# Window attention by quads of four images, with its norm in the loop and its result added to x on the chip

## The chip, the cores and the metric

The program runs on one core of a Trainium2 chip. The metric is the device time of one execution, in microseconds; the time before is the median of three runs. PE is the matrix engine, DVE the vector engine, ACT the activation engine, POOL the general engine; SP and ACT also start DMAs. Each engine works off its own list of instructions in order, and semaphores order the engines among each other. Matrix products land in PSUM, eight banks of 512 f32 columns on 128 lanes.

## The reference

x is f32, 16 images of 24 channels, 56 x 56 pixels. Four layers follow each other; each adds a mixer's result to x and then a feed-forward network's result. Only the first mixer, the norm in front of it and the feed-forward of layer 0 are touched here:

```python
x = x + _L0_conv_ref(_ln_c(x), w_qkv, pos_emb, w_out, b_out)     # attention in 7 x 7 windows
t = _to_tokens(x)
t = t + _L0_ffn_ref(_ln_t(t), W1, b1, W2, b2)                    # rounded to e5m2 and f16
...
# _ln_c: minus the mean, by the standard deviation, over the 24 channels of a pixel
# _L0_conv_ref, per window of 49 pixels and each of 3 heads of 32:
dots = einsum(q, k) * scale + bias[head]                         # 49 x 49
out  = einsum(softmax(dots), v)                                  # then w_out, b_out
```

The other mixers are a selective scan (layer 1), a scan in four directions (layer 2) and an LSTM over rows (layer 3).

## The kernel before

All of x stays in SBUF for the whole program as 128 lanes of J x 3136 columns: lane group g (32 lanes, 24 of them used) holds images g*4 to g*4+3 one after the other. N = 392 columns are 7 rows of 56 pixels, a strip; a chunk of the normalization and of the feed-forward is one strip of four images, one per lane group, and there are 32 of them.

`first_norm_phase` (lines 508 to 644) loads x by 16 DMAs, clears the rest of the lanes, and normalizes 32 chunks with four rings of buffers: PE subtracts the mean by a matrix (L630), ACT squares (L599), PE averages (L637), ACT takes the logarithm and the exponential (L605, L611), DVE multiplies into a padded tile (L585), and SP stores four pieces per chunk to `normed` in DRAM (L559).

`attention_phase` (lines 682 to 1000) takes one image at a time: 128 chunks of 7 rows, 8 windows each. SP loads 24 channels of 7 rows from `normed` (L761); POOL copies them window by window into `xw`, 24 lanes of 128 (L785), after a small instruction that orders it (L780). Under the 24 lanes, lanes 32 to 80 of `xw` hold a one-hot and those of `keys` the position bias, so the product of both over 128 lanes gives scores and bias at once. On PE a chunk is: the keys of three heads (L821, one product of 392 columns), the values of each window (L829, 16 products of 48 columns that alternate between two halves of 64 lanes), the weighing of the values of the chunk two before (L863 and L865, 16 products of 49 columns), the scores (L840, 8 products of 147 columns, windows alternating between the two halves), and the transposes of the probabilities of the chunk before (L851, L853). DVE takes maxima (L958), subtracts (L961), sums (L974), takes reciprocals (L977), lands part of the transposed (L969) and the result with its bias (L983); ACT lands keys (L893), values (L901) and the rest of the transposed (L912), takes exponentials (L906) and stores the result to `mixed` in DRAM (L917); POOL multiplies by the shares (L792). Two buffers of most tiles alternate; the function `slots` writes a prologue, a loop of two chunks a turn, and an epilogue, and the order of calls in each engine's `slot` is the order of its work.

In the trace an f32 matmul is two instructions, a transpose one, and each has its own weight load (PEld).

`feed_forward_phase` (lines 131 to 502) runs once per layer over the 32 chunks, four chunks a turn. SP loads the mixer's result into four `mixed` buffers (L217), POOL adds it to x (`add_mixed`, L360) four chunks ahead and adds the network's result (`update`, L366) when `biased` (L321) is there; DVE rounds and casts (L292 to L315), ACT normalizes, and SP stores the next mixer's normalized input (L243). The order on SP is: store of chunk c, then the loads of chunk c + 6. PE multiplies zeros at the start (L426) and its mean product of chunk c (L441) waits for `added`.

## Time and profile before

| | us |
|---|---|
| median of three runs (3751.98 to 3758.53) | 3753.66 |
| profiled execution, first to last instruction (span) | 3742.5 |
| PE busy, share of the span | 3205.8, 86% |
| DVE | 2806.7, 75% |
| ACT | 2516.9, 67% |
| POOL | 1935.3, 52% |

The span of the profiled execution is 11.2 us shorter than the median of the runs; what lies around it is not in the trace. The kernel passes through stages one after another, so the shares of the whole span say little about one of them. The touched stages end at 1011.5 us. A matmul's duration in the trace includes the time until its last column has landed, so two that follow each other overlap; busy time counts the overlap once.

### The profile page before, as it was taken

How to read it: one execution, taken by the hardware profiler on the slowest of the kernel's cores; microseconds unless marked ns; L12 is line 12 of the kernel's file. 1: busy time of each engine (PE TensorE's matmuls, PEld its weight loads, DVE VectorE, ACT ScalarE, POOL GpSimd, SP SyncE). 2: the span in 40 equal slices, each digit the busy share in tenths (PEclk: the TensorE clock that was granted, in tenths of full speed). 3: DMA queues.
4: the chain of work that ended last, by engine and by line, in shares of the span. 5: the costliest groups of instructions: out<-in, count | busy, mean ns of one | idle time of the engine just before them, and what ended most of it. 6: DMA issues, size and time to landing. Idle time of an engine off the chain costs nothing. (4 is left out here: it accounts for less than half of the span.)

```text
span 3742.5 us, 70954 instructions
## 1 busy us (share of the span) xinstructions
PE 3205.8 (86%) x21002; PEld 1807.7 (48%) x21002; DVE 2806.7 (75%) x4339; ACT 2516.9 (67%) x4557; POOL 1935.3 (52%) x1754
## 2 busy tenths in 40 slices
PE   5799999989787899999999867887999968788877
PEld 2588888864333444444444322333334324377742
DVE  2566666658636999999999997785999968644467
ACT  4455555548676998989998743785767638644456
POOL 0233333323246888889898875333777763200035
PEclk9899999999898999999999999998999989899999
DMA  4100000012256566574747542220000002230022
GB/s 97 30 15 14 14 15 14 14 26 52 71 168 170 144 182 188 160 209 142 211 138 208 140 120 60 56 55 23 21 22 20 20 24 51 72 70 17 17 53 61
DMA packets 211925, 297.93 MB, mean 80 GB/s; under 512 B 68990, under 2 KB 189106, under 8 KB 211382
## 3 DMA queue, kind: packets, MB, share of 16 engines
q1 hardware_dynamic: 204254, 286.98, 28.5%
q10 hardware_dynamic: 7512, 9.16, 0.9%
q8 instruction: 60, 0.98, 0.1%
q14 instruction: 99, 0.81, 0.1%
HBM read 193.93 MB, written 102.03 MB: 79 GB/s over the span
## 5 line engine op out<-in xcount | busy, mean ns | idle before, releaser
L1773 POOL TENSOR_TENSOR mam_hc<-mam_h,mam_cs 128x896 f32<-128x896 f32 x336 | 703.4, 2094 | 166.8 <-DVE mam_h L1692 93.5
L1692 DVE TENSOR_TENSOR_SCAN mam_h<-mam_a,mam_kept,mam_dbx 128x448 f32<-128x448 f32 x672 | 738.3, 1129 | 41.9 <-ACT mam_a L1562 40.9
L1415 PE MATMUL mam_ps_y<-mam_hc,mam_ident 128*128 128x448 f32 x1344 | 569.6, 557 | 125.2 <-POOL mam_hc L1773 124.9
L1562 ACT ACTIVATE mam_a<-mam_ft,mam_a_neg 128x448 f32<-128x448 f32 x672 | 410.8, 660 | 76.7 <-DVE mam_h L1692 75.6
L1415 PEld LDWEIGHTS mam_ps_y<-mam_hc,mam_ident 128*128 128x128 f32 x1344 | 248.5, 192 | 424.7 <-POOL mam_hc L1773 216.2
L792 POOL TENSOR_TENSOR att_prob<-att_prob,att_share 128x588 f32<-128x588 f32 x128 | 151.7, 1185 | 452.1 <-DVE att_share L977 452.1
L1679 DVE TENSOR_TENSOR mam_dbx<-mam_ps_u,mam_bs 128x448 f32<-128x448 f32 x672 | 381.3, 612 | 0.0
L2196 POOL TENSOR_TENSOR scan_ch<-scan_h,scan_cs 128x392 f32<-128x392 f32 x192 | 262.1, 1379 | 61.9 <-DVE scan_h L2138 57.5
L366 POOL TENSOR_TENSOR all_x<-all_x,f_yb 128x392 f32<-128x392 f32 x128 | 128.0, 1000 | 237.2 <-DVE f_yb L321 237.2
L360 POOL TENSOR_TENSOR all_x<-all_x,f_mixed 128x392 f32<-128x392 f32 x128 | 152.5, 1191 | 181.8 <-DMA f_mixed<-mixed 123.6
L912 ACT ACTIVATE att_pt<-att_ps_t 128x512 f32<-128x512 f32 x128 | 76.5, 598 | 209.9 <-PE att_ps_t L853 209.9
L401 ACT ACTIVATE f_h<-f_hid 96x784 f16<-96x784 f32 x256 | 203.1, 808 | 4.5 <-PE f_hid L459 4.3
L893 ACT ACTIVATE att_keys<-att_ps_keys 24x392 f32<-24x392 f32 x384 | 187.0, 487 | 23.0 <-PE att_ps_keys L821 20.0
L2017 PE MATMUL scan_ps_in<-scan_xin,scan_w_in 128*128 128x392 f32 x512 | 189.0, 513 | 12.1 <-DMA scan_xin<-normed 5.4
L354 POOL MEMSET f_squares_ln<- 128x392 f32 x4 | 1.7, 425 | 366.8 <-POOLq L2282 329.6
L863 PE MATMUL att_ps_out<-att_pt,att_vals 128*24 128x49 f32 x2048 | 189.5, 208 | 2.1 <-ACT att_pt L912 2.1
L865 PE MATMUL att_ps_out<-att_pt,att_vals 128*24 128x49 f32 x2048 | 187.3, 207 | 0.0
L2330 PE MATMUL lstm_ps<-lstm_hs,lstm_w_h 64*128 64x224 f32 x1344 | 143.1, 358 | 50.8 <-DVE lstm_hs L2411 50.8
L2029 PE MATMUL scan_ps_merged<-scan_ch,scan_w_merge 64*128 64x392 f32 x768 | 157.7, 521 | 26.8 <-POOL scan_ch L2196 26.8
L310 DVE CAST f_h<-f_hr 96x1568 fp8e5<-96x1568 f16 x128 | 173.3, 1354 | 5.5
L829 PEld LDWEIGHTS att_ps_vals<-att_nvals,att_xw 128*64 128x64 f32 x4096 | 130.5, 138 | 75.5 <-issue 75.5
L983 DVE TENSOR_SCALAR att_result<-att_ps_out,att_b_out 24x392 f32<-24x392 f32 x128 | 78.6, 614 | 115.9 <-PE att_ps_out L865 115.9
(252 smaller groups left out, 7870.8 us busy)
## 6 DMA issues: line engine op xcount, KB each, us to landing
mam_taps<-normed SPq DMA_DIRECT2D x220, 130.5 KB
mam_bs<-dram_bc SPq DMA_DIRECT2D x56, 448.0 KB, 8.8
mam_cs<-dram_bc SPq DMA_DIRECT2D x56, 448.0 KB, 12.0
mam_ft<-dram_steps SPq DMA_DIRECT2D x42, 448.0 KB, 4.8
normed<-f_staged SPq DMA_DIRECT2D x384, 38.1 KB
f_mixed<-mixed SPq DMA_DIRECT2D x384, 36.8 KB
mam_gt<-dram_gs SPq DMA_DIRECT2D x48, 224.0 KB, 2.7
dram_gs<-mam_gs SPq DMA_DIRECT2D x47, 224.0 KB, 2.6
```

The source lines that it names most:

```text
L310: dve.tensor_copy(h8[p][:], hr[:], saturate=False).then_inc(ff["hidden8"], 1)
L401: act.activation(h16[:, 2 * a:2 * a + 2, :], hid[a][0:HID, :, 0:N], ACT.Copy).then_inc(ff["hidden16"], 1)
L863: pe.matmul(ps_out[0:C, cols], vals[p][:, win, 0:C], pt[p][:, q, 64 * half:64 * half + T], start=True, stop=False)
L865: mm = pe.matmul(ps_out[0:C, cols], vals[p][:, win, C:2 * C], pt2[p][:, q, 64 * half:64 * half + T], start=False, stop=True)
L893: o = act.activation(keys[p][0:C, :, h * T:(h + 1) * T], ps_keys[32 * h:32 * h + C, 0:N].rearrange("c (w t) -> c w t", w=WINS), ACT.Copy)
L1415: mm = pe.matmul(ps_y[p % 2][:, 0:MT], ident[:], hc[t % 2][:, i, :], start=False, stop=(t % 8 == 7 and i == 1))
L1562: act.activation(a[t % 3][:, i, :], ft[p % 2][:, 0, :], ACT.Exp, scale=a_neg[:, at:at + 1]).then_inc(decays, 1)
L1679: dve.tensor_tensor(dbx[:, i, 0:MT], ps_u[:, 0:MT], bs[:, held_row(p // DB, pair) + i, :], ALU.mult).then_inc(driven, 1)
L1692: dve.tensor_tensor_scan(h[:, n % 8, :], a[t % 3][:, i, :], dbx[:, i, 0:MT], kept[:, at:at + 1], ALU.mult, ALU.add).then_inc(scanned, 1)
L1773: pool.tensor_tensor(hc[t % 2][:], h[:, row:row + 2, :], cs[:, 2 * pair:2 * pair + 2, :], ALU.mult).then_inc(weighed, 1)
L2017: pe.matmul(ps_in[i][:, 0:N], w_in[:, i, :], xin[p][:, :, 1:SIDE + 1], start=True, stop=True).then_inc(projected, 1)
L2196: pool.tensor_tensor(out, hd, in_order(cs, 1 - half, d, k), ALU.mult).then_inc(weighed, 1)
```

## The change

The phase of the first norm is gone. Attention loads x itself, from an array that the host has laid out by lanes with its padding, in six pieces of 1, 1, 2, 4, 8 and 16 chunks. It takes the 32 chunks of the other phases: a strip of four images at once, each in its own 32 lanes. A unit is half a chunk, four windows of each of four images, so there are 64 units of 16 windows. Norm, keys and windows of chunk c + 1 and c + 2 are made within the units of chunk c. DVE writes the normalized strip straight into the windows `xw`. Keys are one product per head over all lanes, by weights that are zero outside an image's own lanes. Bias and scores are separate products that add up in the same bank; scores and values use 32 lanes of rows and 64 of columns, weighing 64 of rows and 32 of columns. DVE adds the result and its bias to x in SBUF; no result is stored, and nothing is loaded back.

`feed_forward_phase` gets no `mixed` in layer 0 (`in_place`): no loads, no `mixed` buffers, no `add_mixed`, and its mean products don't wait for `added`. The counts of semaphores are shifted to fit.

The diff, cut to its core (the three `slot` functions are those of PE, ACT and DVE, in this order):

```diff
-        first_norm_phase(nc, x, normed, w)
-        for layer in range(LAYERS):
+        attention_phase(nc, w, x, normed)
+        feed_forward_phase(nc, x, None, normed, out_rows, w, st, 0)
+        for layer in range(1, LAYERS):
...
+        ps_s = buf.psum("ps_s", [P, G, BANK])
+        ps_t = [buf.psum(f"ps_t{i}", [P, BANK]) for i in range(2)]
+        ps_l = [buf.psum(f"ps_l{i}", [P, BANK]) for i in range(2)]
...
+        def outs(side):
+            return ps_t[side][:, HEADS * P:HEADS * P + QW * WIN]
...
+                def scores(u, c, e, q):
+                    for g in range(G):
+                        if g % 2 == 0:
+                            reached(pe, shifted, u * 2 + (g // 2 - 1))
+                        lanes = slice(64 * (g % 2), 64 * (g % 2) + TP)
+                        pe.matmul(ps_s[:, g, 0:SCORES], onehot[lanes, :], bias[lanes, :],
+                                  start=True, stop=False)
+                    pe.wait_ge(keys_sb, c * HEADS + HEADS)
+                    for side in range(2):
+                        for g in range(G):
+                            lanes = slice(32 * g, 32 * g + 32)
+                            for half in range(2):
+                                win = 4 * e + 2 * side + half
+                                mm = pe.matmul(
+                                    ps_s[64 * half:64 * half + TP, g, 0:SCORES].rearrange(
+                                        "i (h a j) -> i h a j", h=HEADS, a=2)[:, :, side, :],
+                                    xw[q][lanes, win, :],
+                                    keys[q][lanes, win, :].rearrange("c (h j) -> c h j", h=HEADS),
+                                    start=False, stop=(side == 1))
+                    mm.then_inc(scored, 1)
...
+                def values_product(e, q):
+                    for half in range(2):
+                        for g in range(G):
+                            lanes = slice(32 * g, 32 * g + 32)
+                            for side in range(2):
+                                win = 4 * e + 2 * side + half
+                                at = SCORES + half * VALUES
+                                mm = pe.matmul(
+                                    ps_s[64 * side:64 * side + TP, g, at:at + VALUES],
+                                    xw[q][lanes, win, :], nvals[lanes, :], start=True, stop=True)
...
+                def weigh_values(e, i):
+                    for half in range(2):
+                        for h in range(HEADS):
+                            for g in range(G):
+                                for side in range(2):
+                                    lanes = slice(64 * side, 64 * side + TP)
+                                    mm = pe.matmul(
+                                        outs(side)[32 * g:32 * g + C].rearrange(
+                                            "c (r s) -> c r s", r=WIN)[
+                                                :, :, half * WIN:(half + 1) * WIN],
+                                        vals[i][lanes, g, half, h * C:(h + 1) * C],
+                                        pt[e][lanes, g * HEADS + h, half, :].rearrange(
+                                            "j (r s) -> j r s", r=WIN),
+                                        start=(h == 0), stop=(h == HEADS - 1))
...
+                def turn_probabilities(u, e, g):
+                    if g == 0:
+                        reached(pe, added, u)
+                        pe.wait_ge(normal, u * 2 + 1)
...
+                def slot(u, c, e, q, on):
+                    if on[2]:
+                        scores(u, c, e, q)
+                    if on[4]:
+                        await_probabilities(u - 2)
+                    if on[2]:
+                        values_product(e, q)
+                    if on[4]:
+                        weigh_values(e, (2 * q + e + 2) % 4)
+                    if on[0]:
+                        subtract_mean(c + 2, q)
+                    if on[1]:
+                        keys_product(c + 1, 1 - q, 0)
+                    if on[3]:
+                        turn_probabilities(u - 1, 1 - e, 0)
+                        turn_probabilities(u - 1, 1 - e, 1)
+                    if on[0]:
+                        variance(c + 2, q)
+                    if on[1]:
+                        keys_product(c + 1, 1 - q, 1)
+                    if on[3]:
+                        turn_probabilities(u - 1, 1 - e, 2)
+                        turn_probabilities(u - 1, 1 - e, 3)
+                    if on[1]:
+                        keys_product(c + 1, 1 - q, 2)
+                    if isinstance(u, int) and u == 1:
+                        for piece in range(len(PIECES) - 1):
+                            pe.wait_ge(x_in[piece], 16)
...
+                def slot(u, c, e, q, on):
+                    if on[2]:
+                        take_values(u, 2 * q + e)
+                    if on[0]:
+                        square(c + 2, q)
+                    if on[1]:
+                        take_keys(c + 1, 1 - q, 0)
+                    if on[3]:
+                        take_turned(u - 1, 1 - e, 0)
+                        take_turned(u - 1, 1 - e, 1)
+                    if on[1]:
+                        take_keys(c + 1, 1 - q, 1)
+                    if on[2]:
+                        exponentials(u, e)
+                    if on[0]:
+                        inverse_deviation(c + 2, q)
+                    if on[3]:
+                        take_turned(u - 1, 1 - e, 3)
+                    if on[1]:
+                        take_keys(c + 1, 1 - q, 2)
...
+                def slot(u, c, e, q, on):
+                    if on[3]:
+                        sums(u - 1, 1 - e)
+                    if on[1]:
+                        window(c + 1, 1 - q)
+                    if on[2]:
+                        find_maximum(u, 0)
+                    if on[4]:
+                        add(u - 2, c - 1, e)
+                    if on[2]:
+                        find_maximum(u, 1)
+                        subtract_maximum(u, e, 0)
+                        subtract_maximum(u, e, 1)
+                    if on[3]:
+                        take_turned(u - 1, 1 - e)
```

on[0] holds in every odd unit, on[1] in every even one; the loop's turn is four units. `reached` waits until a semaphore has a value, and does nothing for a constant of zero or less.

## Rows read from the trace of the kernel before

**Rows 1.** Windows by stage: stretch and length, each engine's busy us (instructions), clock, DMA.

```profile
0.00:109.60 109.60, 54.44 (x128) 23.62 (x128) 25.19 (x40) 46.29 (x97) 5.56 (x6) 0.94 0.40 93
109.60:125.30 15.70, 3.90 (x46) 2.66 (x46) 6.16 (x15) 1.48 (x3) 1.50 (x6) 0.50 0.21 59
125.30:821.70 696.40, 690.71 (x11492) 573.24 (x11488) 478.55 (x768) 403.52 (x765) 242.75 (x506) 1.00 0.06 14
821.70:1011.50 189.80, 162.21 (x630) 74.30 (x630) 143.91 (x304) 146.43 (x257) 65.12 (x65) 0.97 0.22 54
```

**Rows 2.** Waits of attention, the longest: us in total, times, longest.

```profile
POOL att_prob L792 <- DVE att_share L977: 452.1, 128, 8.2
```

**Rows 3.** Timeline of PE in one chunk: start us, duration us, instruction, count.

```profile
400.97 0.25 PE L865 MATMUL att_ps_out<-att_pt,att_vals 128*24 128x49 f32 x2
401.15 1.22 PE L840 MATMUL att_ps_scores<-att_keys,att_xw 128*64 128x147 f32 x16
402.30 0.33 PE L851 MATMUL att_ps_t<-att_ident,att_prob 128*128 128x128 f32 x1
...
403.12 0.27 PE L853 MATMUL att_ps_t<-att_ident,att_prob 128*64 128x128 f32 x1
403.23 0.82 PE L821 MATMUL att_ps_keys<-att_xw,att_mkeys 128*96 128x392 f32 x2
403.98 1.14 PE L829 MATMUL att_ps_vals<-att_nvals,att_xw 128*64 128x48 f32 x32
```

**Rows 4.** Groups by form, 400 to 800 us: busy us, mean ns of one.

```profile
L792 POOL TENSOR_TENSOR att_prob<-att_prob,att_share 128x588 f32<-128x588 f32 x74 | 87.7, 1185 | 258.4 <-DVE att_share L977 258.4
...
L974 DVE TENSOR_REDUCE att_total<-att_prob 128x12 f32<-128x588 f32 x75 | 57.5, 766 | 14.4 <-ACT att_prob L906 14.4
L961 DVE TENSOR_TENSOR att_prob<-att_ps_scores,att_top 128x588 f32<-128x588 f32 x74 | 57.2, 773 | 2.5
L958 DVE TENSOR_REDUCE att_top<-att_ps_scores 128x12 f32<-128x588 f32 x74 | 57.0, 770 | 36.9 <-PE att_ps_scores L840 36.9
L906 ACT ACTIVATE att_prob<-att_prob 128x588 f32<-128x588 f32 x74 | 52.7, 712 | 0.0
L969 DVE COPY att_pt<-att_ps_t 64x512 f32<-64x512 f32 x74 | 49.8, 672 | 0.0
...
L983 DVE TENSOR_SCALAR att_result<-att_ps_out,att_b_out 24x392 f32<-24x392 f32 x74 | 45.4, 614 | 66.9 <-PE att_ps_out L865 66.9
...
L977 DVE RECIPROCAL att_share<-att_total 128x12 f32<-128x12 f32 x75 | 17.1, 228 | 2.6
```

**Rows 5.** Bins of 10 ns: PE instructions in flight, first L840, then L863.

```profile
136.54:136.55 0.01, 0.00 (x1) 1.00 0.00 0
136.55:136.56 0.01, 0.01 (x2) 1.00 0.00 0
...
405.05:405.06 0.01, 0.01 (x1) 1.00 0.00 0
405.11:405.12 0.01, 0.01 (x2) 1.00 0.00 0
```

**Rows 6.** Timeline of PE in one row of the LSTM.

```profile
3400.83 2.55 PE L2330 MATMUL lstm_ps<-lstm_hs,lstm_w_h 64*128 64x224 f32 x24 [0.93 <-DVE lstm_hs L2411]
```

**Rows 7.** Timeline of PE in the first chunk of attention.

```profile
123.59 1.95 PE L829 MATMUL att_ps_vals<-att_nvals,att_xw 128*64 128x48 f32 x32
```

**Rows 8.** First norm: its products and results (first start us), and x's load.

```profile
L630 PE MATMUL n_xc<-all_x,n_centre x64: 492/582/1019, 14.2 to 99.2; 128*128 128x392 f32 x64
L585 DVE TENSOR_TENSOR n_staged<-n_xc,n_rstd x32: 567/568/569, 21.1 to 103.8; 128x392 f32<-128x392 f32 x32
...
4.00:33.00 29.00, 12.91 (x30) 6.08 (x30) 6.76 (x12) 8.96 (x19) 2.11 (x1) 1.00 0.75 162
```

**Rows 9.** Waits in the feed-forward of layer 0, 840 to 1000 us.

```profile
POOL all_x L360 <- DMA f_mixed<-mixed: 49.2, 26, 3.0
...
PE f_xc_ff L441 <- POOL all_x L360: 9.2, 20, 0.9
```

More of the change, by code:

```diff
@@ new lines, in attention_phase @@
+        bias = buf.sbuf("bias", [P, SCORES])
+        eps_c = buf.sbuf("eps_c", [P, 1])
+        zeros = buf.sbuf("zeros", [P, PAD + 4])
+        mkeys = buf.sbuf("mkeys", [P, HEADS, P])
+        nvals = buf.sbuf("nvals", [P, VALUES])
+        squares = buf.sbuf("squares", [P, N])
+        rstd = buf.sbuf("rstd", [P, N])
+        xw = [buf.sbuf(f"xw{q}", [P, WINS, TP]) for q in range(2)]
+        keys = [buf.sbuf(f"keys{q}", [P, WINS, HT]) for q in range(2)]
+        vals = [buf.sbuf(f"vals{i}", [P, G, 2, VALUES]) for i in range(4)]
@@ L766, in _, with load @@
-                for p in range(2):
-                    sp.wait_ge(left[p], 16 * chunks // 2)
+                sp.dma_start(centre[:], w["centre"]).then_inc(weights_in, 16)
+                sp.dma_start(average[:], w["average"]).then_inc(weights_in, 16)
+                def load(i):
+                    at = slice(PIECES[i] * N, PIECES[i + 1] * N)
+                    sp.dma_start(x[:, at], w["x"][:, at]).then_inc(x_in[i], 16)
+                load(0)
+                for tile, name in ((wq, "att_wq"), (wk, "att_wk"), (wv, "att_wv"), (wo, "att_wo")):
+                    sp.dma_start(tile[:], w[name]).then_inc(weights_in, 16)
@@ new lines, in _ @@
+                load(1)
+                for tile, name in ((onehot, "att_onehot"), (bias, "att_bias"), (ident, "ident"),
+                                   (b_out, "att_b")):
+                    sp.dma_start(tile[:], w[name]).then_inc(weights_in, 16)
+                for i in range(2, len(PIECES) - 1):
+                    load(i)
+                sp.wait_ge(zeroed, 1)
+                rows = normed.rearrange("b c n -> (b c) n").rearrange("(i r) n -> i r n", i=3)
+                R = rows.shape[1]
@@ L804, in _, with normalize @@
-                normalize(chunks - 2, 0)
-                normalize(chunks - 1, 1)
+                for e in range(2):
+                    pool.memset(prob[e][:], 0.0).then_inc(set_up, 1)
+                pool.wait_ge(set_up, 10)
+                def normalize(u, e):
+                    pool.wait_ge(shared, u + 1)
+                    for part in range(2):
+                        at = slice(part * PAIRED_TURNS, (part + 1) * PAIRED_TURNS)
+                        pool.tensor_tensor(
+                            prob[e][:, at, 0:T], prob[e][:, at, 0:T],
+                            share[e][:, at].unsqueeze(2).to_broadcast([P, PAIRED_TURNS, T]),
+                            ALU.mult).then_inc(normal, 1)
@@ L835, in scores @@
-                def scores(c, p):
-                    pe.wait_ge(keys_sb, c + 1)
-                    reached(pe, shifted, c)
-                    for win in range(WINS):
-                        q, half = win // 2, win % 2
-                        mm = pe.matmul(ps_scores[64 * half:64 * half + TP, q // 2,
-                                                 (q % 2) * HT:(q % 2 + 1) * HT],
-                                       xw[p][:, win, :], keys[p][:, win, :], start=True, stop=True)
-                    mm.then_inc(scored, 1)
@@ L909, in take_turned @@
[L909 to L920 removed]
+                load_exp_and_ln(nc)
@@ new lines, in add @@
+                def add(u, c, e):
+                    dve.wait_ge(mixed_up, u + 1)
+                    rows = x[:, bass.ds(c * N, N)].rearrange("c (r s) -> c r s", r=WIN)
+                    for side in range(2):
+                        at = slice((2 * e + side) * QW, (2 * e + side + 1) * QW)
+                        op = dve.scalar_tensor_tensor(
+                            rows[:, :, at], outs(side).rearrange("c (r s) -> c r s", r=WIN),
+                            b_out[:, 0:1], rows[:, :, at], ALU.add, ALU.add)
+                    op.then_inc(added, 1)
```

576 lines of the change are left out of this document (222 added, 354 removed).

## The prediction, made before the changed kernel was run

> **What bounds the kernel now.** I read the windows by stage first [rows 1]: the first normalization fills 0 to 109.6 us, set-up and the first chunk go to 125.3, attention runs to 821.7, the feed-forward of layer 0 to 1011.5. Nothing later is touched, so the question is what 1011.5 becomes. In attention PE is busy 690.7 of 696.4 us at a granted clock of 1.00; DVE (478.6), ACT (403.5) and POOL (242.8) are not. The waits, second, agree: POOL sat 452.1 us behind DVE's shares [rows 2], and that engine delays nobody. So attention costs what PE's stream costs: 696.4 / 128 = 5.44 us a chunk of 8 windows, 10.9 us for 16 windows, the unit of the new loop.
>
> The timeline of one chunk, third, splits that [rows 3]. An f32 product is two matmul instructions. The last two weighing instructions start about 44 ns apart (0.25 us for both, 0.21 for one), 49 columns each. Scores: 16 of 147 columns in 1.22 us with a tail of about 0.29, so (1.22 - 0.29) / 15 = 62 ns. Transposes: 8 in 403.23 - 402.30, about 0.11 each. Keys: 2 of 392 columns, the second 0.33 behind the first. Values: 32 of 48 columns in 1.14 us with a tail of 0.22, so 29 ns. Where the tile's shape changes lies about 0.1 us: keys stream until 403.23 + 0.66 = 403.89, values begin at 403.98.
>
> **What one instruction streams.** Keys give 0.33 / 392 = 0.84 ns a column, weighing 44 / 49 = 0.9. Scores should then take 147 x 0.84 = 123 ns and come every 62: their two windows lie on two column halves of the array. Bins of 10 ns show it: a scores group has its second instruction in flight within 10 ns of the first, while weighing, all on one tile, has its second 60 ns later [rows 5]. Row halves do the same in the LSTM: 24 instructions of 224 columns (188 ns each) in 2.55 - 0.35 us, 92 ns apart [rows 6]. So halves run side by side in either direction, which proves a factor of two. Four row groups, and rows combined with columns, no row of before shows.
>
> **The change part by part.** Quads of images put four row groups (K = 32) with two column halves under scores and values, and tiles of 64 x 32 under weighing: eight tiles each. Per unit of 16 windows PE issues:
> - Bias: 4 products, 8 instructions of 294 columns on two row halves: 8 x 294 x 0.84 / 2 = 0.99 us.
> - Scores: 32 instructions. Streams spread over 8 tiles would be 32 x 123 / 8 = 0.49; over two 1.97; serial 3.94.
> - Values: 32 instructions of 72 columns: 0.24, 0.97 or 1.94.
> - Weighing: 96 instructions of 49 columns: 0.53, 2.11 or 4.22 (96 x 44).
> - Keys 3 and norm 2 products per two units: 5 x 2 x 0.33 / 2 = 1.65 (the norm's two are the old phase's, moved into the loop).
> - Transposes: 12 at 0.107 = 1.29 (16 before).
> - Changes of tile shape: 5 at 0.1 = 0.5.
>
> What spacing do eight tiles reach? The shortest that PE shows is the values' 29 ns; at the start of attention, at a clock of half speed, the same group took 1.95 us, 56 ns [rows 7], so it follows the array's clock and is no limit of issue. On average 11492 matmul instructions left in 696.4 us, one per 60.6 ns [rows 1]. So the spacing of the 160 small instructions lies between an eighth of a stream (8 ns) and 60 ns; I take 28, from the nearest row. Then scores 0.90, values 0.90, weighing 2.69, in all 0.99 + 0.90 + 0.90 + 2.69 + 1.65 + 1.29 + 0.5 = 8.92 us. At 8 ns it is 6.0 (scores 0.49, values 0.26, weighing 0.77), at 60 ns and 185 instructions 11.1.
>
> Added waits. There is one score buffer, so a unit's scores wait for `shifted` of the unit before, with all of PE queued behind; DVE puts `add`, which waits for weighing, between the two maxima. From the start of scores: 0.90 + 0.90 + 0.1 + 2.69 + 0.2 to land = 4.8. Maximum and subtractions keep their shape, 0.77 each; the add is two of 98 elements, by its nearest row (0.61 for 392) 0.2 to 0.6 in all, I take 0.6 [rows 4]. 4.8 + 0.6 + 3 x 0.8 = 7.8, then 0.05, half the bias (0.5) and 0.1 to the next scores: 8.45, half a us under PE. DVE alone: sums of 1176 elements 1.38, share 0.25, maxima and subtractions 4 x 0.77, the norm's product 0.57 every other unit, one image of the transposed 0.45, add 0.6: 6.05, with the exponential between subtraction and sums about 6.6. POOL: 2 x 1.19. ACT lands 3 groups of keys where it landed 12 (four chunks' worth for a strip of four images), so it stays below its old 2 x 3.15 plus 0.72 for the norm (46.3 / 64) [rows 1, 4]. Transposing waits for `added`, because results share its bank: landing 0.2 + add 0.6 against 0.65 of keys or norm in between, 0.1 of stall at most. Before weighing PE waits for ACT's last landing of the unit before; where the norm's logarithm and exponential (two of its three steps on ACT, 46.3 / 32 = 1.45 us, so about 1.0) stand ahead of it, it comes some 2.5 us into the slot and PE is there at 2.0: 0.5 every other unit, 0.25 each. So 9.17 us a unit, 64 x 9.17 = 587.
>
> - Start. The norm phase with its block end goes (109.6 us), its 128 stores, the 128 loads of rows and ACT's 128 stores too. The memsets lie beside the weights' landing; the six edge DMAs move behind x on SP, and nobody waits for them before the block's end. Left: two pieces of x and ten weights, 0.9 MB at the 162 GB/s of the old load [rows 8], so PE starts at about 10; folding 2.5; one chunk's norm 6.9 (first product 14.2, first result 21.1 [rows 8]); keys 4.5: scores begin at 24. After the second unit PE waits for all of x: 6.4 MB (padding is loaded now) and the 0.9 end at about 47, the second unit at 24 + 18 = 42; I add 3 of the 5: 27.
> - End. The last unit's exponential, sums, share, POOL, transposes, landing, weighing, add: 0.7 + 1.4 + 0.3 + 2.4 + 0.4 + 0.4 + 2.7 + 0.6 and hand-overs: 10. Attention ends at 27 + 587 + 10 = 624 instead of 821.7.
> - Feed-forward. `add_mixed`, its 128 loads ahead of SP's stores and four memsets go. Those loads made POOL wait 49.2 us, but PE only 9.2 us for POOL [rows 9]; late next are PE's own order and DVE's cast. Bounds 0 to -16, taken -6.
>
> Sum: 3742.5 - 198 - 6 = 3538.5 us of span; the median of the runs, 3753.66, lies 11.2 above the profiled span, kept: **3550 us**.
>
> TensorE: Matmul & The Clock Gate in the Trainium skill (Part 3, Packing small matmuls) says that matmuls on different row and column groups overlap, 16 tiles having measured 10.6 times one; for two, [rows 5, 6] agree. That rule gives the second rival. Part 1 of that page of the Trainium skill ("Wait — 56ns, not 53.3ns?") says that a sequencer decoding in software spends about 62 ns on a matmul, which would make 185 x 62 = 11.5 us a unit, an estimate from that page; the 60.6 ns of [rows 1] neither reach nor exclude it. That rule speaks against the change and stands beside the first rival.
>
> **The rivals.**
> 1. Issue limits PE. 185 instructions per unit stand against 180 before: if 60 ns is the sequencer's own pace, unseen so far because the array needed as much, a unit takes 11.1 us: 710 + 37 = 747, time 3753.7 - 75 - 6 = 3673. For: the average of 60.6. Against: the gaps in a chunk sit only where the tile's shape changes, and 64 instructions of values and weighing follow at 29 and 44 ns.
> 2. Eight tiles overlap and issue is free. PE falls to 6.0, and DVE's ring (sums, maxima, add, subtractions, exponential) sets 6.6 to 7: 64 x 6.7 = 429 + 37 = 466, time 3753.7 - 356 - 6 = 3392. For: [rows 5]. Against: nothing below 28 ns was seen.
> 3. Slower: groups of 32 rows don't run side by side, neither over rows nor with columns. Then 0.99 + 3.94 + 1.94 + 4.22 + 1.65 + 1.29 + 0.5 = 14.5 us a unit, 930 + 37 = 967, time 3893. It decides from (821.7 + 6 - 37) / 64 = 12.4 us a unit. For: K was 128 for these products before; a group of 32 rows streams as many columns for a quarter of the sums. Against: [rows 5, 6].
>
> **How the numbers follow.** Forecast 0.50 (units of 8 to 9.8 us, 3475 to 3590), issue 0.22, free tiles 0.20, slower 0.08. The range 3395 to 3680 reaches over the first two rivals and leaves out the slower one and the ends. A measurement here tells 0.2% (7.5 us) from no change: faster 0.91, within 0.01, slower 0.08.
>
> **What would show it.** First scores at 24 to 27 us; a unit of 9.2 us, weighing's 96 instructions in 2.7; PE busy over 90% of the loop at a granted clock of 1.00; attention's end near 624; feed-forward 184 us. Weighing in 5 us with even spacing means issue; PE idle before the bias products, behind DVE's subtraction, means the ring. Over 12.4 us a unit the forecast is wrong in sign.

## The result, and the profile after

The changed kernel took 3383.23 us (median of 4 runs, 3380.93 to 3388.71) against 3752.82 for the kernel before on the same chip: a ratio of 0.9023, 95% interval 0.9007 to 0.9039. The forecast was 3550, its range 3395 to 3680: the sign was right, the gain almost twice as large, and the time 12 us below the range. The span of the profiled execution is 3379.3 us, 3.9 below the median. The forecast kept 11.2 us between the two, as before; but a run's time is only 1.6 us longer than its own span (3380.93 for 3379.3), so most of the 11.2 presumably lay in the profiled execution of before having been faster than the median. 7 of the 167 us between forecast and time are this.

First the windows by stage of the changed kernel, as in [rows 1]: stretch and length, each engine's busy us (instructions) for PE, PEld, DVE, ACT, POOL, then clock, DMA share, GB/s. The stages are the start up to the first bias products, the loop, its end, and the feed-forward of layer 0.

```profile
0.00:23.70 23.70, 10.61 (x62) 5.12 (x62) 3.96 (x17) 4.90 (x8) 2.90 (x6) 1.00 0.82 296
23.70:447.90 424.20, 417.66 (x11449) 287.90 (x11450) 352.70 (x591) 276.13 (x622) 144.26 (x124) 1.00 0.00 1
447.90:462.70 14.80, 9.66 (x382) 7.36 (x378) 8.45 (x16) 4.84 (x12) 4.65 (x4) 0.84 0.02 5
462.70:643.00 180.30, 166.18 (x630) 72.20 (x630) 134.14 (x299) 142.54 (x255) 30.15 (x33) 0.96 0.12 30
```

Almost as many matmul instructions as before (11449 for 11492) pass in 424 us instead of 696. The values of the first unit begin at 25.45 us and those of the last at 449.02, so a unit takes 423.57 / 63 = 6.72 us, where 9.17 was forecast. Against the forecast's terms in us:

| term | forecast | after |
|---|---|---|
| start | 27 | 23.7 |
| 64 units | 587 | 430 |
| end | 10 | 9 |
| attention ends at | 624 | 462.7 |
| feed-forward of layer 0 | 189.8 - 6 | 180.3 |
| everything later | 2731.0 | 2736.3 |

The unit is nearly the whole error: 64 x (9.17 - 6.72) = 157 of the 159 us by which the span is shorter than forecast. Second, PE's timeline through one unit, as in [rows 3]: start us, duration us, instruction, tile rows*columns, shape, count.

```profile
205.32 1.26 PE L721 MATMUL att_ps_s<-att_bias,att_onehot 64*128 64x294 f32 x8
206.51 0.76 PE L729 MATMUL att_ps_s<-att_keys,att_xw 32*64 32x147 f32 x32
207.06 0.62 PE L745 MATMUL att_ps_s<-att_nvals,att_xw 32*64 32x72 f32 x32
207.62 1.07 PE L762 MATMUL att_ps_t<-att_pt,att_vals 64*24 64x49 f32 x96
208.65 0.92 PE L696 MATMUL att_ps_l<-all_x,att_centre 128*128 x2
209.55 0.87 PE L783 MATMUL att_ps_t<-att_ident,att_prob 128*128 128x128 f32 x6
210.26 0.91 PE L703 MATMUL att_ps_l<-att_squares,att_average 128*128 128x392 f32 x2
211.00 0.82 PE L783 MATMUL att_ps_t<-att_ident,att_prob 128*128 128x128 f32 x6
211.75 1.26 PE L721 MATMUL att_ps_s<-att_bias,att_onehot 64*128 64x294 f32 x8
```

The starts give the prices: bias 1.19, scores 0.55, values 0.56, weighing 1.03, the norm's two products and the transposes 3.10 together, 6.43 in all (a slot with three keys products in their place takes about 7). The forecast had for such a slot 0.99, 0.90, 0.90, 2.69 and 1.32 + 1.29 + 0.5 = 3.11. So each sum is within 0.2 us except the 160 small instructions: 2.14 us where 4.49 stood. (The starts put a change of tile shape into the price of the group ahead of it, and the 3.10 holds a stall, told of below.) Within a group: the 96 of the weighing last 1.07 us, of which some 0.21 are the tail of one, so (1.07 - 0.21) / 95 = 9.1 ns apart; on the one tile of [rows 3] they were 44 ns apart.

Third, the waits of the loop, 100 to 400 us: engine, its line <- whom; us in total, times, longest. POOL's wait answers to [rows 2].

```profile
POOL att_prob L667 <- DVE att_share L959: 199.0, 45, 4.8
ACT att_vals L852 <- PE att_ps_s L745: 44.5, 45, 1.3
DVE att_total L955 <- ACT att_prob L860: 26.1, 44, 0.9
PEld att_ps_t L783 <- POOL att_prob L667: 21.2, 34, 0.7
DVE att_top L927 <- ACT att_vals L852: 14.7, 34, 0.6
```

And the groups by form that answer to [rows 4]: busy us, mean ns of one. DVE's add (L967) costs two times 312 ns, the 0.6 us that the forecast took; DVE is busy 84% of the loop (251.8 us of these 300), PE 298.7.

```profile
L927 DVE TENSOR_REDUCE att_top<-att_ps_s 128x12 f32<-128x588 f32 x90 | 68.9, 766 | 16.3 <-ACT att_vals L852 14.7
L955 DVE TENSOR_REDUCE att_total<-att_prob 128x24 f32<-128x1176 f32 x44 | 60.6, 1378 | 26.1 <-ACT att_prob L860 26.1
L967 DVE SCALAR_TENSOR_TENSOR all_x<-att_ps_t,att_b_out,all_x 128x98 f32 x90 | 24.5, 312 | 0.0
```

So two readings were open. The time agrees with the second rival (3392), which put the bound on DVE's ring; PE's rows, second, show no idle time at all. One more thing is to be seen in PE's rows: from the first product behind the weighing (208.65) to the transposes (209.55) lie 0.90 us, while such a product takes 0.66 elsewhere in the loop (keys from 203.25, transposes behind them from 203.91). The view books the rest as busy, since the product's duration of 0.92 covers it. At 209.55 the add has just ended (next fence, DVE and ACT in the same slot).

```profile
207.72 0.71 ACT L852 ACTIVATE att_vals<-att_ps_s 128x288 f32<-128x288 f32 x2 [1.25 <-PE att_ps_s L745]
208.17 0.77 DVE L927 TENSOR_REDUCE att_top<-att_ps_s 128x12 f32<-128x588 f32 x1 [0.55 <-ACT att_vals L852]
208.85 0.57 DVE L967 SCALAR_TENSOR_TENSOR all_x<-att_ps_t,att_b_out,all_x 128x98 f32 x2
209.34 0.76 DVE L927 TENSOR_REDUCE att_top<-att_ps_s 128x12 f32<-128x588 f32 x1
```

### The profile page after: what moved, and what is told of

The parts are those of the page before. It is cut to its first block and busy times, and to the rows that moved or that the text cites. A ratio compares the mean times of both kernels' runs of the same rounds, so it can differ in the third digit from the quotient of the medians.

```text
span 3379.3 us, 68245 instructions
## 1 busy us (share of the span) xinstructions
PE 2896.7 (86%) x21230; PEld 1503.5 (44%) x21230; DVE 2655.7 (79%) x4136; ACT 2342.8 (69%) x4333; POOL 1802.1 (53%) x1338
## 5 line engine op out<-in xcount | busy, mean ns | idle before, releaser
L366 POOL TENSOR_TENSOR all_x<-all_x,f_mixed 128x392 f32<-128x392 f32 x96 | 119.3, 1242 | 126.3 <-DMA f_mixed<-mixed 67.3
L316 DVE CAST f_h<-f_hr 96x1568 fp8e5<-96x1568 f16 x128 | 162.9, 1273 | 5.4
L305 DVE TENSOR_SCALAR f_hr<-f_h,f_b 96x784 f16<-96x784 f16 x256 | 150.4, 588 | 20.2 <-ACT f_h L407 16.2
L2184 POOL TENSOR_TENSOR scan_ch_first<-scan_h,scan_cs 128x392 f32<-128x392 f32 x64 | 104.6, 1634 | 114.2 <-DVE scan_h L2126 107.2
L2126 DVE TENSOR_TENSOR_SCAN scan_h<-scan_decay_by_column,scan_h,scan_drive_by_column 128x392 f32<-128x392 f32 x112 | 162.7, 1452 | 0.0
L1350 PE MATMUL mam_ps_a<-mam_taps,mam_win 120*128 120x448 f32 x224 | 106.9, 602 | 60.9 <-DMA mam_taps<-normed 57.1
L2318 PEld LDWEIGHTS lstm_ps<-lstm_hs,lstm_w_h 64*128 64x128 f32 x1344 | 123.6, 185 | 70.3 <-DVE lstm_hs L2399 69.9
L2126 DVE TENSOR_TENSOR_SCAN scan_h<-scan_decay,scan_h,scan_drive 128x392 f32<-128x392 f32 x112 | 153.8, 1412 | 0.6
```

Of the source, the lines that this page charges most:

```text
L316: dve.tensor_copy(h8[p][:], hr[:], saturate=False).then_inc(ff["hidden8"], 1)
L2126: dve.tensor_tensor_scan(out, a, v, before, ALU.mult, ALU.add).then_inc(scanned, 1)
L2184: pool.tensor_tensor(out, hd, in_order(cs, 1 - half, d, k), ALU.mult).then_inc(weighed, 1)
L2318: mm = pe.matmul(ps[p][:, pair, half, 0:W], w_h[lanes, tap, pair, :], hs[lanes, :, y, tap:tap + SIDE], start=False, stop=(tap == 2))
```

## The experiments

Each is the changed kernel with the edit shown; differences are between medians, against 3383.2 us, and the ratio stands to the kernel before, which took 3748 to 3751 us beside these runs and 3753 beside the changed kernel. So a difference of a few us tells nothing by itself. Theory A: tiles work side by side, the small instructions follow 9 ns apart, and PE's queue sets the unit. Theory B: DVE's own work sets it. Theory C came after the run with half the weighing.

**The order of the small instructions.**

```diff
-                    for half in range(2):
-                        for h in range(HEADS):
-                            for g in range(G):
-                                for side in range(2):
+                    for g in range(G):
+                        for side in range(2):
+                            for half in range(2):
+                                for h in range(HEADS):
```

> The weighing's 96 small products per unit go out tile by tile (12 on one 64x32 tile, then 12 on the next) instead of one for each of the eight tiles in turn; the arithmetic is the same. In the changed kernel 96 of them end within 1.07 us, 9.1 ns apart. If that spacing comes from eight tiles that work side by side, products of one tile stand one behind another, about 44 ns each (128 columns of a 32-column tile's stream of the scores' and values' kind: 32 in 0.76 us over 4 row groups). If TensorE looks only at its nearest neighbours in the queue: 96 x 44 ns = 4.2 us in place of 0.87, 3.3 us per unit, 64 units, +211 us: about 3594 us. If it looks some tens of instructions ahead (two or three tiles in flight): 1.5 us, +41 us: about 3424. If each tile had a queue of its own as deep as twelve: no change, 3383 to 3400.

Measured: 3518.96 us, ratio 0.9387 (0.9371 to 0.9403), +136 us or 2.1 us a unit. PE's timeline of this run:

```profile
207.38 0.62 PE L745 MATMUL att_ps_s<-att_nvals,att_xw 32*64 32x72 f32 x32
207.94 3.29 PE L762 MATMUL att_ps_t<-att_pt,att_vals 64*24 64x49 f32 x96
211.16 0.93 PE L696 MATMUL att_ps_l<-all_x,att_centre 128*128 x2
```

The same 96 instructions take 3.29 us in place of 1.07, (3.29 - 0.21) / 95 = 32 ns apart. The truth lies between the first two answers. 32 is less than the 44 ns of one tile, so some overlap between neighbours seems to be left; but of the two orders only the one that changes the tile with every product (two instructions) gives the 9 ns. This run is close to what the forecast assumed of the weighing (28 ns), and its time is near the forecast's.

**Twice the weighing.**

```diff
+                    for _ in range(2):
                         for half in range(2):
                             for h in range(HEADS):
```

> The weighing's 96 products are issued twice (the second pass begins its sums anew, so the result stands); nothing is added to any other engine. This measures the disputed price by itself. Theory A (tiles side by side, small products about 9 ns apart, and TensorE's queue in order sets the unit): 96 x 9.1 ns = 0.87 us per unit, x 64 = +56 us: about 3439 us. Theory B (VectorE's ring of sums, maxima, add and subtractions sets the 6.7 us of a unit, TensorE has room): under half of it shows, 3383 to 3405. The prediction's own price for 96 products, 2.69 us: +172 us, 3555.

Measured: 3632.2 us, ratio 0.9690 (0.9673 to 0.9707), +249 us: no answer was right. PE's timeline, and the DMA view of 100 to 400 us (queue, kind: packets, MB, share of 16 engines):

```profile
203.65 0.82 PE L784 MATMUL att_ps_t<-att_ident,att_prob 128*128 128x128 f32 x6
208.09 2.33 PE L721 MATMUL att_ps_s<-att_bias,att_onehot 64*128 64x294 f32 x8 [3.62 <-issue]
...
243.37 0.96 PE L763 MATMUL att_ps_t<-att_pt,att_vals 64*24 64x49 f32 x82
244.79 1.20 PE L763 MATMUL att_ps_t<-att_pt,att_vals 64*24 64x49 f32 x110 [0.46 <-issue]
...
q8 instruction: 69, 1.13, 1.6%
```

The instructions themselves keep their price, (1.20 - 0.21) / 109 = 9.1 ns. But PE now stands for up to 3.6 us with nothing to wait for in the profile, and 69 packets of instructions were loaded in these 300 us; the changed kernel loaded none there:

```profile
DMA packets 0, 0.00 MB, mean 0 GB/s; under 512 B 0, under 2 KB 0, under 8 KB 0
```

After this longest gap PE ran at the lower clock for a while: the granted clock was 0.55 from 208 to 215 us, behind 4 us with 0.47 us of PE's work, and the bias products took 2.33 us instead of 1.26. Over the 300 us it was 0.91. So this run shows another cost, told of in the last section, and not the price of the weighing in its place.

**More PE, more DVE.** Two products of 392 columns per chunk (not 512, as the expectation has it) are issued twice (the first run), or the second maximum is taken twice (the second run):

```diff
-                    pe.matmul(ps_l[1 - q][:, 0:N], average[:], squares[:],
-                              start=True, stop=True).then_inc(varied, 1)
+                    for _ in range(2):
+                        mm = pe.matmul(ps_l[1 - q][:, 0:N], average[:], squares[:],
+                                       start=True, stop=True)
+                    mm.then_inc(varied, 1)
...
-                    pe.matmul(ps_l[(q + h) % 2][:, 0:N], mkeys[:, h, :], xw[q][:, :, 0:T],
-                              start=True, stop=True).then_inc(keyed, 1)
+                    for _ in range(2 if h == 2 else 1):
+                        mm = pe.matmul(ps_l[(q + h) % 2][:, 0:N], mkeys[:, h, :], xw[q][:, :, 0:T],
+                                       start=True, stop=True)
+                    mm.then_inc(keyed, 1)
```

> Two products of 512 columns per chunk of two units are issued twice, the variance and the third keys product (0.65 us each): 0.65 us more of TensorE per unit, away from the ring that VectorE and ScalarE run on (both are followed by slack there). Theory A (TensorE's order sets the unit): 64 x 0.65 = +42 us, about 3425 us. Theory B (VectorE's ring sets it): 0 to +10 us, 3383 to 3393.

```diff
+                    if pair == 1:
+                        reached(dve, topped, u * 2 + 1)
+                        dve.tensor_reduce(
+                            again[:],
+                            ps_s[:, images, 0:SCORES].rearrange("i g (n j) -> i g n j", j=T),
+                            AX.X, ALU.max)
```

> VectorE takes the second of a unit's two maxima twice (the first time into a tile that nobody reads): 0.77 us more of VectorE per unit, nothing more on TensorE. Theory A (TensorE's order sets the unit; VectorE is 84% busy, so about 1.1 us of a unit's 6.7 are free on it): the most of it goes into VectorE's idle time, +6 to +13 us by later work, 3390 to 3396 us. Theory B (VectorE's ring sets it): 64 x 0.77 = +49 us, about 3432 us.

Measured: 3419.33 us, ratio 0.9117 (0.9104 to 0.9130), +36 for 0.65 us of PE a unit; 3403.89 us, ratio 0.9079 (0.9064 to 0.9095), +21 for 0.77 us of DVE. PE counts nearly in full (0.56 of 0.65), DVE by less than half (0.32 of 0.77), though by more than the +6 to +13 of theory A. What PE waits for now is ACT's last landing of the transposed, which stands ahead of the values. The first line is this run's, the second the changed kernel's:

```profile
PE att_ps_s L746 <- ACT att_pt L868: 13.0, 21, 0.7
PEld att_ps_s L745 <- ACT att_pt L867: 1.6, 9, 0.2
```

13.0 / 42 = 0.31 us a unit, all of it in the slots with the norm: there DVE's later subtraction makes ACT's exponentials later, behind these stand the norm's logarithm and exponential, and behind these the landing. So the changed kernel has next to nothing in reserve on this way; its own rows:

```profile
212.94 0.76 PE L729 MATMUL att_ps_s<-att_keys,att_xw 32*64 32x147 f32 x32
213.13 0.40 ACT L867 ACTIVATE att_pt<-att_ps_t 128x294 f32<-128x294 f32 x1
213.58 0.54 PE L745 MATMUL att_ps_s<-att_nvals,att_xw 32*64 32x72 f32 x32
```

The next bias, for its part, loses nothing by the later subtraction: its weight loads stood 14.1 us for "issue" and 1.8 for DVE before, and stand 1.9 and 16.0 now. Theory B is out, since DVE's work alone would count in full and PE's not at all. A holds for work late in PE's slot.

**Orders that were to help.** The second keys product ahead of the first transposes on PE (first run), and the exponentials ahead of the second keys copy on ACT (second run):

```diff
                         keys_product(c + 1, 1 - q, 0)
+                        keys_product(c + 1, 1 - q, 1)
                     if on[3]:
                         turn_probabilities(u - 1, 1 - e, 0)
...
-                    if on[1]:
-                        keys_product(c + 1, 1 - q, 1)
```

> On TensorE the second keys product goes out ahead of the first two images' transposes instead of behind them, in the slots that have keys products (every second one). There the first transposes come 0.3 us late now, held until VectorE has added the last unit's outputs to x; with 0.65 us of other work ahead of them they find that done. Theory A: 0.3 us less in 32 of the 64 units, -10 us, about 3374 us. Theory B (VectorE's ring sets the unit): 0, or a little slower by the later transposes, 3383 to 3390.

```diff
-                    if on[1]:
-                        take_keys(c + 1, 1 - q, 1)
                     if on[2]:
                         exponentials(u, e)
+                    if on[1]:
+                        take_keys(c + 1, 1 - q, 1)
```

> On ScalarE the exponentials go out ahead of the second keys copy instead of behind it. Now they begin 0.4 to 0.8 us after their subtraction is done in every second slot, and VectorE stands 0.9 us before its sums there, against 0.2 us in the other slots. Theory A (TensorE's order sets the unit): within 4 us of 3383. Theory B (VectorE's ring sets it): 0.7 us less in 32 units, -20 us, about 3362 us.

Measured: 3388.47 us, ratio 0.9038 (0.9024 to 0.9052), and 3383.12 us, ratio 0.9027 (0.9014 to 0.9041). The first missed (+5 for -10; the intervals overlap, so that it is slower isn't shown): with nothing left between the two pairs of transposes, the second pair now waits for ACT to land the first, which has its bank:

```profile
PEld att_ps_t L783 <- ACT att_pt L866: 9.1, 22, 0.4
```

The second did nothing, as A said and against B. DVE's wait ahead of its sums fell from 26.1 to 12.7 us and its wait ahead of the first maximum rose from 14.7 to 28.7: DVE's idle time only moved.

**Half the weighing**, the outputs of the second half of the rows left stale:

```diff
-                    for half in range(2):
+                    for half in range(1):
```

> The weighing is left out for the second half of the rows (48 of a unit's 96 small products; their outputs are stale). This measures the small products' price without more instructions in the loop, which in the run with the weighing issued twice were fetched again and again. Theory A with 9.1 ns each: 48 x 9.1 ns = 0.44 us per unit, x 64 = -28 us, about 3355 us. Theory B: 0 to -5 us, 3378 to 3383. At the prediction's 28 ns: -86 us, 3297.

Measured: 3381.29 us, ratio 0.9029 (0.9011 to 0.9046): nothing gained, against A. PE's busy time fell to 280.5 of 300 us, and what it saved it spends in this wait:

```profile
PE att_ps_t L783 <- DVE all_x L967: 19.0, 45, 0.5
```

Theory C follows from it: the transposes wait for the add, because the weighed results share their bank, and two paths of nearly equal length lead from the values' products to the add. One is PE's (weighing), the other goes over ACT's copy of the values and DVE's first maximum, behind which the add stands. With transposes, norm or keys, bias, scores and values behind it, this is a ring over three engines, one turn a unit: in the rows of after 207.72 (copy), 208.17 (maximum), 208.85 (add), 209.55 (transposes), 211.75 (bias), and at 214.20, 6.48 us after the first, the next copy. Four runs test it.

```diff
-                    if on[4]:
-                        add(u - 2, c - 1, e)
                     if on[2]:
                         find_maximum(u, 1)
+                    if on[4]:
+                        add(u - 2, c - 1, e)
```

> VectorE adds a unit's outputs to x behind both maxima instead of between them; no engine gets more work. Theory C (the unit is set by a ring over three engines: values' products, ScalarE's copy of them 0.45 us, VectorE's first maximum 0.7, add 0.7, then on TensorE transposes, keys or variance, transposes, bias, scores, values): the add ends 0.77 us later and so do the transposes, 64 x 0.77 = +49 us, about 3432 us. Theory B (VectorE's own work sets it): 0 to -10 us, 3373 to 3383. A plain sum over TensorE's queue (theory A without the wait): 0.

```diff
# ScalarE, take_values; the weighing is cut to half as above
+                    for pair in (1, 0):
+                        if pair == 1:
+                            act.wait_ge(valued, u + 1)
+                        else:
+                            act.wait_ge(topped, u * 2 + 1)
# VectorE, find_maximum
+                    if pair == 0:
+                        dve.wait_ge(valued, u + 1)
+                    else:
+                        dve.wait_ge(vals_sb, u * 2 + 1)
# VectorE, subtract_maximum of pair 0
+                        dve.wait_ge(vals_sb, u * 2 + 2)
```

> Two edits. The weighing is left out for the second half of the rows (48 of 96 small products, outputs stale), which alone changed nothing; and the first maximum no longer waits for ScalarE's copy of the values: VectorE takes it first, while ScalarE copies the other two images, then they change places. Theory C: between values and the first transposes two paths of nearly equal length stand side by side, TensorE's (weighing, then the add) and ScalarE's and VectorE's (copy, maximum, add); with both shorter by about 0.4 us the unit follows, 64 x 0.3 to 0.44 = -19 to -28 us, 3355 to 3364 us. Theory B (VectorE's own work): 0 to -8 us.

```diff
# PE: the weighing between scores and values, its wait ahead of the scores
# DVE:
                     if on[4]:
                         add(u - 2, c - 1, e)
                     if on[2]:
                         find_maximum(u, 0)
                         find_maximum(u, 1)
```

> TensorE weighs the values of the unit before last ahead of the new unit's values product instead of behind it, and VectorE adds the result to x ahead of both maxima. The add is then done before the first transposes are due, so their stall of 0.3 us per unit goes. Theory C: the ring through the add is cut; but the maxima begin about 0.2 to 0.7 us later, and the subtractions release the next bias. -10 to -18 us where there is room (3365 to 3373), up to +20 where the subtractions become the new ring (3403). Theory B (VectorE's own work): 0.

```diff
# nvals is widened to [P, G, VALUES], zero outside an image's own lanes
-                                    xw[q][lanes, win, :], nvals[lanes, :], start=True, stop=True)
+                                    xw[q][:, win, :], nvals[:, g, :], start=True, stop=True)
```

> The values products are taken off the row groups: each of the 32 uses all 128 rows of the array with the other images' rows of the weights zero (the same result), so that no two images' products run side by side; spacing then by the stream of 72 columns on tiles that share all rows, about 30 to 35 ns each by the tile-by-tile weighing (33 ns), against some 10 to 17 now. 32 x 17 to 25 ns = 0.5 to 0.8 us per unit, all on the ring (theory C) and on TensorE's queue (theory A): +35 to +51 us, 3418 to 3434 us. Theory B: 0 to +10 us.

Measured, in this order: 3419.01 us, ratio 0.9127 (0.9110 to 0.9143), +36; 3361.79, 0.8961 (0.8943 to 0.8978), -21; 3423.63, 0.9129 (0.9113 to 0.9145), +40; 3426.60, 0.9143 (0.9125 to 0.9162), +43. Moving the add with no work added cost 0.56 us a unit, and PE stood 0.65 us for it; cutting both paths gave 0.33 us a unit, where cutting PE's alone gave nothing. Both are C and neither B, nor A without the wait. The run without row groups came as both A and C said, and speaks against B alone. The values without row groups take 1.22 us in place of 0.62, 32 ns apart. From the first, the third and the fourth of these runs, PE's rows:

```profile
203.44 0.87 PE L783 MATMUL att_ps_t<-att_ident,att_prob 128*128 128x128 f32 x6 [0.65 <-DVE all_x L967]
```

```profile
202.00 0.76 PE L731 MATMUL att_ps_s<-att_keys,att_xw 32*64 32x147 f32 x32 [1.19 <-ACT att_pt L869]
```

```profile
203.14 1.22 PE L744 MATMUL att_ps_s<-att_nvals,att_xw 128*64 128x72 f32 x32
204.29 1.07 PE L761 MATMUL att_ps_t<-att_pt,att_vals 64*24 64x49 f32 x96
```

The weighing ahead of the values missed for another reason than the one feared: with it, the wait for ACT's last landing moved up ahead of the scores, and in every second slot that landing stands behind the logarithm and exponential of the norm:

```profile
PE att_ps_s L731 <- ACT att_pt L869: 26.7, 21, 1.4
```

26.7 / 42 = 0.64 us a unit, as much as the run lost (0.63). It is the wait for which the forecast put 0.25 us a unit, and which the changed kernel just escapes because bias and scores come first.

**What was left open: the small instructions' price, and a faster version.**

```diff
-                    for half in range(2):
+                    for half in (0, 0, 1):
```

> The weighing's first half is issued twice (48 small instructions more per unit, 9.1 ns each in the trace; the result stands). If the loop's instructions still stay on the chip: 0.44 us more on TensorE's path from the values to the add, of which 0.1 to 0.2 us fall into the slack that the maximum's path leaves: 64 x 0.25 to 0.35 = +16 to +22 us, 3399 to 3405. At 28 ns each: 1.34 us, +75 us, 3458. If the loop's instructions are fetched again as in the run with the whole weighing twice: instruction packets in the loop, gaps of 1 to 4 us, +60 to +150 us.

The next is the edit of the run with both paths cut, without the cut of the weighing; the last adds to it:

> Only the second edit of the run with the two: the first maximum doesn't wait for ScalarE's copy of the values. Theory C: the maximum's path is 0.4 us shorter, and TensorE's path (weighing, add) then holds the first transposes, 0.1 us earlier in one slot and 0.2 in the next: 64 x 0.15 = -10 us, about 3373 us. Theory B: 0.

```diff
                         keys_product(c + 1, 1 - q, 0)
+                        keys_product(c + 1, 1 - q, 1)
                     if on[3]:
                         turn_probabilities(u - 1, 1 - e, 0)
...
-                        keys_product(c + 1, 1 - q, 1)
+                        keys_product(c + 1, 1 - q, 2)
                     if on[3]:
                         turn_probabilities(u - 1, 1 - e, 2)
...
-                    if on[1]:
-                        keys_product(c + 1, 1 - q, 2)
```

> As the run with the maximum first, and on TensorE the keys products stand ahead of each pair of transposes: first, second, transposes of two images, third, transposes of the other two. Theory C: in every second slot the transposes then find the add done, 0.3 us less, and 0.1 in the others: 64 x 0.2 = -13 us, about 3370 us. If the later transposes hold ScalarE's copies and VectorE's sums instead: 0 to +8, 3383 to 3391.

Measured: 3504.68 us, ratio 0.9343 (0.9318 to 0.9367), +121; 3378.89, 0.9017 (0.9005 to 0.9029), -4; 3374.74, 0.9002 (0.8990 to 0.9014), -8. With half as much weighing again the loop's instructions are loaded anew already, and PE stands for them:

```profile
q8 instruction: 77, 1.26, 1.7%
```

```profile
PE att_ps_s L721 <- issue: 22.5, 9, 3.2
PE att_ps_t L762 <- issue: 19.2, 20, 1.8
```

So adding instructions can't price them here. Taking them away can, once the other path is short: between the run with the maximum first and the one with half the weighing as well lie 17 us (21 by the ratios), 0.27 us a unit for 48 instructions or 5.6 ns each; that the rest up to the 9.1 ns of the trace falls into the path beside it is likely and not shown. At 28 ns the 48 would have been worth 1.34 us a unit.

The maximum first alone gave less than C said (-4 for -10, and by the intervals perhaps nothing), since the weighing and the add behind it then hold the transposes nearly as late. In that run the add waits for PE's weighing in every second slot, and 0.89 us still lie between the product and the transposes:

```profile
DVE all_x L974 <- PE att_ps_t L762: 8.0, 24, 0.3
206.56 0.92 PE L696 MATMUL att_ps_l<-all_x,att_centre 128*128 x2
207.45 0.87 PE L783 MATMUL att_ps_t<-att_ident,att_prob 128*128 128x128 f32 x6
```

With the keys ahead it is the fastest that computes all, 8 us under the changed kernel by the medians; the intervals of the two ratios (0.8990 to 0.9014, 0.9007 to 0.9039) overlap a little, so that it is faster than the changed kernel is likely and not shown. That it beats the kernel before is.

## Why the prediction was right in sign and too small

- The step that failed is "I take 28, from the nearest row": the spacing of the 160 small instructions. They are 9.1 ns (weighing), 13 (values, (0.62 - 0.22) / 31) and 15 (scores, (0.76 - 0.28) / 31) apart, with the changes of tile in all 2.14 us a unit for the 4.49 of the forecast. That is 64 x 2.35 = 150 of the 157 us. The end of 8 ns that the forecast worked out and set aside, 6.0 us of PE a unit, lies 0.7 under the 6.72 measured, and 0.25 of this is a stall. The mistake is in what the row can say: the values' 29 ns came from two tiles, and [rows 5] had already shown that two start together. A spacing reached on two tiles was no floor for eight. The scores show it best: 62 ns on two tiles before, 15 on eight, a quarter. The same quarter of 29 would have been 7. Not every group comes that low: an eighth of the 44 ns that the weighing took on one tile is 5.5, and what holds it at 9.1 no run shows. The run with the weighing tile by tile shows the other half: where the order doesn't spread the tiles, 32 ns do stand.
- The 60.6 ns on average of [rows 1], the first rival's ground, was no pace of issue: it is 424.20 / 11449 = 37 ns now, and 9.1 in the weighing. TensorE: Matmul & The Clock Gate in the Trainium skill (Part 1, "Wait — 56ns, not 53.3ns?") gives some 62 ns for a matmul decoded in software; the 9.1 ns of the trace speak against that here.
- The second rival had the number (3392, measured 3383) and half of the mechanism, so its number is in part luck. Tiles do overlap, and issue at 60 ns doesn't hold them; but DVE's work doesn't set the unit, since 0.77 us more of it cost 0.32, and moving the add without adding work cost 0.56. A ring through PE, ACT and DVE does, with PE's own order equally long beside it.
- The stall on the add was forecast as 0.1 us at most; it is 0.25 (0.90 for 0.65). PE's path alone makes that much: in the run with the maximum first the weighing ends at 206.6, the add ends 0.7 later, at 207.3, and the transposes begin at 207.45, 0.89 for 0.65. The forecast had left out the hand-over behind the add. That the other path, over ACT's copy and the first maximum, ends at the same time it didn't see.
- The 0.25 us for ACT's late landing nearly didn't come, but only just: in the slots with the norm the landing ends at 213.53 and the values begin at 213.58, with 0.64 us between scores and values for 0.55 in the other slots. The run with the second maximum taken twice shows what 0.77 us less reserve costs there.
- Bias was 0.2 too cheap: its eight instructions take 1.19 us and not 0.99. Norm, transposes and changes of shape came to 3.10 for 3.11, but that is luck: 0.25 of the 3.10 is the stall, which the forecast had elsewhere. A large product alone carried over from the rows of before (0.66 for 2 x 0.33).
- Start (first bias products at 23.7 for 24; the 3 us added for the rest of x show nowhere, no PE instruction waits for it), end (9 for 10) and feed-forward (-9.5 for -6) came close. In the feed-forward no PE instruction waits for POOL any more but the first (1.4 us; before, 3.1 there and the 9.2 of [rows 9]); POOL has 30.2 us of work there, 65.1 before.

## What to carry to other kernels

A spacing read from instructions that share the array by two was an upper end for eight here: work out one instruction's stream divided by the tiles that the new order keeps in flight, give it a real chance, and look whether neighbours in the queue lie on different tiles; the order alone was worth 136 us. Where an engine's saved work brings nothing, look for a path of equal length beside it and shorten both in one run: half the weighing gave 0 alone and 17 us beside the shorter path. And where an engine is slowed to test it, look at what PE then waits for: DVE's work reached PE here through ACT. Before a loop is unrolled or filled up further, see whether its instructions are loaded again in each pass.

## What the runs showed of the hardware that was not expected

The changed loop has (11449 + 11450) / 63.1 = 363 matmuls and weight loads a unit, 1452 in a pass of four units, and no instruction packets in the loop. With 96 more a unit (some 1840 a pass) there were 77 packets in 300 us, and with 192 more (some 2220) 69: about nine and ten of 16 KB in each pass. PE stood up to 3.6 us at the loop's bias products and up to 2.3 us amid the weighing, and these two runs took 121 and 249 us more for 28 and 56 us of added work. Nothing in the changed kernel's own profile says how near it is.

Runtime: NRT & Kernel Launch in the Trainium skill (Instruction fetch mechanics) says that PE holds 2048 instructions and refills by blocks of 16 KiB, that a kernel needn't fit since the loading is mostly hidden, and that a branch to a page outside the window that is held must wait for its fetch. The size of the packets (1.26 MB / 77 = 16.4 KB) and the gaps agree; "mostly hidden" doesn't in these two loops, and the loading began somewhere between 1452 and 1840 recorded instructions a pass, beside those that the trace doesn't record.
